# FFN chunks of three blocks in place of four in a fused graph layer and FFN kernel

## The reference

```python
x = x + gnn(layernorm(x), src, dst, ...)
    # neigh = segment_sum(x[src], dst) / max(deg, 1)
    # h = x @ W_self + b_self + neigh @ W_neigh
    # h = layernorm(h) * gamma + beta; h = where(h >= 0, h, alpha * h); return h + x
x = x + ffn(layernorm(x))
    # gate, up = x @ Wg.T, x @ Wu.T            (512 -> 1408)
    # down = (silu(gate) * up) @ Wd.T          (1408 -> 512)
    # each W is ternary in groups of 128 inputs: {-1, 0, 1} * scale of the group
```

## Time and profile before

| | us |
|---|---|
| median of 3 runs | 1665.63 (1665.43 to 1667.83) |
| the profiled execution | 1666.25 |
| its span in the profile | 1664.2 |
| TensorE busy | 1575.4 |
| VectorE busy | 1102.3 |
| ScalarE busy | 1027.2 |
| GpSimd busy | 1009.4 |

### The profile page before, as it was taken

One profiled execution on the slowest core, in us unless ns is written; L12 is line 12 of the kernel. 1 busy time (PEld: TensorE's weight loads), 2 busy tenths in 40 slices (PEclk: granted clock), 3 DMA queues, 4 the chain that ended last, 5 costly groups with the idle time before them and its releaser, 6 DMA issues.

```text
span 1664.2 us, 23257 instructions
## 1 busy us (share of the span) xinstructions
PE 1575.4 (95%) x7582; PEld 845.1 (51%) x7583; DVE 1102.3 (66%) x2408; ACT 1027.2 (62%) x1735; POOL 1009.4 (61%) x985
## 2 busy tenths in 40 slices
PE   6799899979988999999999999999999999999897
PEld 3344444434555455555555555555555555555342
DVE  6478586414466677767677776767777676766875
ACT  2232234400046777777777777777777777777786
POOL 2233343357777777777777777777777777774000
PEclk9899999999999999999999999999999999999999
DMA  9645344368987777787787877777777777874000
GB/s 342 234 162 190 147 151 156 116 240 281 313 252 228 235 223 228 231 247 227 218 247 223 244 223 242 233 212 249 221 231 232 239 225 209 250 227 146 0 26 25
DMA packets 132952, 346.30 MB, mean 208 GB/s; under 512 B 32776, under 2 KB 32776, under 8 KB 132822
## 3 DMA queue, kind: packets, MB, share of 16 engines
q0 software_dynamic: 70560, 231.27, 46.4%
q1 hardware_dynamic: 62272, 113.54, 19.5%
HBM read 287.97 MB, written 57.18 MB: 207 GB/s over the span
## 4 chain that ended last, share of the span: by engine, by line
PE 76%; issue 6%; POOL 5%; DMA 5%; SPq 3%; DVE 3%; ACT 2%; ACTq 0%; DVEq 0%; POOLq 0%
PE f_ps L759 19%; PE f_ps L760 19%; PE f_ps L607 13%; PE agg_ps L691 12%; PE agg_ps L693 9%; POOL rows L559 4%; DMA own_rows<-work 3%; PE tr_ps L710 1%; PE out_ps L719 1%; DMA rows<-node_table,idx 1%; DMA own_rows<-hsx 1%; SPq L406 1%; SPq L359 1%; DVE acc L1156 1%; POOL hsx L544 1%
## 5 line engine op out<-in xcount | busy, mean ns | idle before, releaser
L559 POOL DMA_INDIRECT rows<-node_table,idx x882 | 897.5, 1018 | 287.8 <-issue 258.3
L844 ACT ACTIVATE f_ps<-f_ps,ratio 128x512 f32<-128x512 f32 (+1 forms) x1068 | 648.3, 635 | 225.5 <-PE f_ps L760 215.1
L759 PE MATMUL f_ps<-x1T,tern 128*128 128x512 f16 (+1 forms) x1144 | 415.3, 367 | 10.2 <-DVE f_ps L1148 5.0
L760 PE MATMUL f_ps<-x1T,tern 128*128 128x512 f16 (+1 forms) x1144 | 414.9, 367 | 0.0
L691 PE MATMUL agg_ps<-rows,hot 128*128 128x512 f16 x846 | 350.3, 414 | 0.0
L1148 DVE TENSOR_SCALAR f_ps<-f_ps,ratio 128x512 f32<-128x512 f32 (+1 forms) x310 | 225.2, 728 | 170.0 <-PE f_ps L760 167.3
L693 PE MATMUL agg_ps<-rows,hot 128*128 128x512 f16 x846 | 322.2, 381 | 0.0
L759 PE MATMUL f_ps<-hT,tern 128*128 128x512 f16 (+1 forms) x572 | 207.3, 367 | 2.0 <-DVE f_ps L1148 1.3
L760 PE MATMUL f_ps<-hT,tern 128*128 128x512 f16 (+1 forms) x572 | 207.2, 367 | 0.0
L1156 DVE SCALAR_TENSOR_TENSOR acc<-f_ps,scl,acc 128x512 f32<-128x512 f32 (+1 forms) x143 | 102.9, 720 | 139.0 <-PE f_ps L760 81.3
L690 PEld LDWEIGHTS deg_ps<-ones,hot 128*128 128x128 f16 x846 | 119.4, 141 | 122.3 <-issue 24.0
(11 more groups left out here) (167 smaller groups left out, 1860.4 us busy)
## 6 DMA issues: line engine op xcount, KB each, us to landing
hsx<-own_rows SPq DMA_DIRECT2D x49, 512.0 KB, 5.6
own_rows<-hsx SPq DMA_DIRECT2D x30, 512.0 KB, 3.4
rows<-node_table,idx POOLq DMA_INDIRECT x882, 4.1
node_table<-work SPq DMA_DIRECT2D x49, 256.0 KB, 2.1
out_nodes<-work SPq DMA_DIRECT2D x48, 256.0 KB, 3.8
rows<-in_x SPq DMA_DIRECT2D x3, 1792.0 KB, 8.6
own_rows<-bias_b SPq DMA_DIRECT2D x1, 4864.0 KB, 22.1
own_rows<-hsx SPq DMA_DIRECT2D x19, 256.0 KB, 2.3
```

Source lines behind the costliest of these rows:

```text
L559: pool.indirect_dma_start(out=rows[:, j, :], out_offset=None, in_=table[:, :], in_offset=bass.IndirectOffsetOnAxis(ap=of[:, j:j + 1], axis ...
L759: pe.matmul(to, lhs, parts[0], start=g == 0, stop=False, skip_group_check=True)
L760: pe.matmul(to, lhs, parts[1], start=False, stop=True, skip_group_check=True).then_inc(p_ff, 1)
L844: act.activation(ps, ps, ACT.Copy, scale=ratio[:, w if up else 2, j:j + 1]).then_inc(a_scaled, 1)
```

## The change

The twelve chunks of four blocks become sixteen chunks of three, 384 columns. Chunk 0 is spread over 1.3 slots in place of 2.3, and chunk 1 begins at position 6.4 in place of 7.4. A step then moves the position by 3/132, which gives 44 steps a slot; the last step lies at 54.42. Chunk c needs block 3c, ready in slot 3c + 2, and begins at 3c + 3.4. All that is derived from the step order (which engine scales, when halves are made, transposes and adds) follows.

```diff
-    SIZE = [1] + [4] * 12
+    SIZE = [1] + [3] * 16
...
-        if c == 1 and pos < 7.4:
-            pos = 7.4
+        if c == 1 and pos < 6.4:
+            pos = 6.4
         t, k = int(pos), int((pos - int(pos)) * TICKS)
         AT.setdefault((t, k), []).append(s)
-        pos += 2.3 / 132 if c == 0 else SIZE[c] / 132.0
+        pos += 1.3 / 132 if c == 0 else SIZE[c] / 132.0
```

## The result

The changed kernel takes 1691.45 us (median of 4 runs, 1690.02 to 1693.26), the kernel before beside it 1666.73 us: 1.0148 times as long, 95% interval 1.0131 to 1.0166. It is 25 us slower. The forecast was 6 us slower, with a range up to 1688; the direction was right, the size was not, and the range missed it by 3 us.

The account below looks back on a forecast made before the run. TensorE was taken to bound the settled middle, gathers a close second, with gains only at the ends. End -11, start +6, middle matmuls +2 and stalls +9 made +6 on the 1665.63 median: 1671.6 us, range 1657 to 1688.

Parts of the forecast that it names:

- What bounds the kernel: Whole kernel: TensorE is the bound between 576 and 1544 us, with 8.6 us of stalls; only the two ends can gain.
- The end: FFN steps after the sums: less matmul time and one add fewer, partly offset by more non-matmul time; -11 us.
- The start: Slots 5 to 8: squeezed chunk 0 waits on a bank's loop, slots 7 and 8 give back 4; +6 us.
- Matmuls in the middle: Middle slots: 88 matmuls of 0.163 us against 66 of 0.216 a slot, over 40 slots; +2 us.
- The sums end: Sign in the profile after: the sums' end, shortly before 1544 us, comes 15 to 18 us later if the forecast holds.
- The rule that a weight load overlaps a matmul only with other row groups: Rival for all FFN matmuls: 1056 additional weight loads come into the open, 103 us, 1769 us; 1 in 100.
- Stalls at slot starts: First sums of middle slots wait for VectorE's read in 13 slots instead of seven, 8 us instead of 4; +4 us.
- the steps' own waits: Middle slots: FFN steps wait for their bank as its room falls to 0.58 us; 0.1 to 0.2 us a slot, +5.
- both kinds of stall together: Middle slots: slot-start stalls plus steps' waits, +9 us; +2 if queues stay short, +22 if each slot loses 0.55 more.
- Rival D: Eviction engines become the bound in the slots, each losing 0.7 us more; +29 us in all, 1695 us; 12 in 100.

Follow-up runs that it names:

- thin pair: Changed kernel and kernel before, each with every scaling between groups cut to 2 columns, beside a before of 1666 us: 1653.2 and 1645.7 us.
- e7: Changed kernel with every scaling on ScalarE while there are sums; ratio to before 1.0101.
- e15: Kernel before, four blocks, sizes and counts unchanged, with the steps of each three ticks issued together; 1783.95 us, ratio 1.0710.
- e18: Kernel before with chunk 1 from position 6.9 and chunk 0 over 1.8 slots, old rule for VectorE's scalings; ratio 1.0027.
- e17: Kernel before with chunk 1 from position 6.9, chunk 0 over 1.8 slots, VectorE's scalings only in calm ticks; 1656.4 us, ratio 0.9948.
- e14: Kernel before with every scaling between groups cut to 2 columns, beside a before of 1666 us; 1645.7 us, ratio 0.9880.
- e4: Kernel before with scalings between groups cut to 2 columns, beside a before of 1856 us; two such runs took 1836.4 and 1837.9 us.
- e1: Kernel before with chunks of three blocks, old start kept, beside a before of 1856 us; 1947.6 us, ratio 1.0489.
- e2: Kernel before, chunks of four, only chunk 0 squeezed into 1.3 slots, beside a before of 1856 us; 1869.4 us, ratio 1.0060.

## Why the prediction missed, point by point

**What bounds the kernel** held: the middle is TensorE's, and only the ends had something to give. **The end**, -11 us, measured -10.3. The FFN after the sums takes 96.9 us from 24 us after slot 48's start to the last step, where I had written 97; what is not matmul in it grew from some 16 to 21 us, and I had 19.6. **The start**, +6, measured +7.5, and its parts came as written: slot 5 takes 30.0 us (28.5 forecast), slot 6 24.6 (25), and slots 7 and 8 give back 3.7 (4). The length of the scalings is only part of it: in the thin pair slot 5 still takes 27.7 us against 20.9; the rest I did not trace. **Matmuls in the middle**, +2, measured +2.8. The sums end 38 us later (1580 in place of 1542), where I had written 15 to 18; that is the same miss as in the middle.

The rule that a weight load overlaps a matmul only with other row groups (the Trainium skill, TensorE: Matmul & The Clock Gate, Part 3: Packing small matmuls) would have added 103 us. With starts 0.163 us apart and a load between each pair, the trace contradicts it at this width as well. The same section of the Trainium skill also lets a load that targets the background weight buffer be pulled ahead, and with that the trace agrees.

**Stalls at slot starts**: I counted 13 slots in the step order and took 8 us in place of 4. They measure 9.3 in place of 4.4, and twelve of my slots have one of 0.4 to 0.9 us ahead of the first sums (11, 13, 18, 22, 25, 26, 31, 33, 37, 41, 43 and 48); in slot 19 the 1.4 us wait just ahead of the sums covers it. Slots 14 and 44, with a scaling and a low half in tick 0, have 0.6 each and were not on the list. For the kernel before I had counted seven; its trace has eight (9, 10, 27 to 30, 47, 48).

**The step that failed** is the last term, "the steps' own waits". I worked out that a bank's room falls from 1.25 us to 0.58, and wrote that I take 0.1 to 0.2 us a slot, +5. It measures +18.1 us, 0.46 us a slot. The mechanism was right; its size was set by feeling, as the text admits, and the upper bound for both kinds of stall together, +22, lay just under the +22.9 that came. Two things in the working pulled it down. I treated 0.58 us as the room of every second return; at the start of a slot there are seven steps without sums, where a bank comes back after 1.30 us against a loop of 1.21, which I had used only for the end. 10.7 of L759's 19.5 us fall on steps of ticks 1 and 2. And I took 0.1 to 0.2 us a slot where eleven single waits alone, of 0.6 to 1.4 us each, make 0.25 us a slot. Rival D (+28 us in the slots, at 12 in 100) had the size, and with the norm and `one_hot` the place of the long waits. But it made the engines the bound, which e7 and e15 speak against: more load on ScalarE made the kernel 8 us faster, and in e15 the same load as before stalls L759 for 27 us.

Open is how much of the 19.5 us another order of steps and sums inside a tick would win back; that was not tried.

## What to carry to other kernels

A smaller tile with the same total costs almost nothing in columns (2.8 us here) and hides that every buffer comes back sooner: the pass over it shrinks only to 0.82 (VectorE's scaling takes 0.622 us at 384 columns against 0.756 at 512), the time of the four steps until it is wanted to 0.75 (1.30 us against 1.73). So price the room between the two at its narrowest place, not on average, and multiply by everything that stands behind the waiting instruction. And before moving a schedule by a fraction of a period, count which operations fall in front of the one read that frees a single buffer: here that count, with a start chosen by it, turned a useless shift (1.0027) into a gain (0.9948). It gave 4 to 6 us between e18 and e17, and 13 came, 10 of them stalls of the first sums: such a count is a lower bound.

## What the runs showed of the hardware

The thin four-block kernel was traced at 1645 us (e14) and at 1833 us (e4). The 188 us between them lie in the slots with gathers: L759's stalls in slots 9 to 47 are 121 us in e4 and 0 in e14, while slot 48 to the end is the same (132.6 and 132.6 us). In e4 ScalarE, VectorE and GpSimd start late without a reason that shows on their own core; the trace gives such waits the releaser "remote". 111 of them are longer than 1 us, in e14 none is. The longest of ScalarE's is 6.8 us; one of 4.7 looks like this:

```profile
674.90 0.39 ACT L844 ACTIVATE f_ps<-f_ps,ratio 128x2 f32<-128x2 f32 x2 [4.70 <-remote]
...
675.19 0.39 PE L759 MATMUL f_ps<-hT,tern 128*128 128x512 f16 x1 [2.43 <-ACT f_ps L844]
```

They all lie between 380 and 1697 us, in the slots in which GpSimd gathers; what delays the engines was not settled. There the narrower room is dearer still: three-block chunks lose 93 us in the middle (e1 against e2) in place of 26.
